# A graph layer with halving weights on one Trainium2 core: one-tile units at both ends, marks chosen per unit, counts alternating with products, and bases by VectorE scans

## The reference

```python
def reference(x, adj, L0_gnn_weight, L0_gnn_bias):      # x (4096, 64), adj (4096, 4096) of 0.0 and 1.0, fp32
    h = jnp.maximum(_layernorm(x, axis=-1), 0.0)
    support = h @ weight                                # (4096, 64)
    mask = (adj != 0).astype(support.dtype)
    rank = jnp.cumsum(mask, axis=1)
    deg = rank[:, -1:]
    k = jnp.minimum(deg, 100.0)
    pos = rank - (deg - k)
    w = mask * jnp.where(pos > 0, 0.5 ** (k - pos), 0.0)
    return x + (w @ support + bias)
```

## Time and profile before

| | before |
|---|---|
| median of 3 runs | 245.06 us (244.77 to 246.62) |
| profiled execution | 244.41 us, its span 242.1 us |
| PE, PEld | 208.9 us (86%), 203.0 us (84%) |
| DVE | 206.9 us (85%) |
| ACT | 170.2 us (70%) |
| POOL | 31.3 us (13%) |
| adjacency loads | 33.56 MB written, 67.1% of the 16 DMA engines' span |
| granted TensorE clock, mean | 0.979 |

### The profile page before, as it was taken

One profiled execution on the slowest core, in us unless ns is written; L12 is line 12 of the kernel. 1 busy time (PEld: TensorE's weight loads), 2 busy tenths in 40 slices (PEclk: granted clock), 3 DMA queues, 4 the chain that ended last, 5 costly groups with the idle time before them and its releaser, 6 DMA issues.

```text
span 242.1 us, 6387 instructions
## 1 busy us (share of the span) xinstructions
PE 208.9 (86%) x2816; PEld 203.0 (84%) x2816; DVE 206.9 (85%) x285; ACT 170.2 (70%) x302; POOL 31.3 (13%) x53
## 2 busy tenths in 40 slices
PE   0530766886999999999999999999999999999993
PEld 0530654776998999999999999999999999999982
DVE  0999979999999999999998999998999995526424
ACT  2411636856687888787888887888887888888640
POOL 8500000004001040104040104030000000000000
PEclk9995699999999999999999999999999999999999
DMA  7999999999999999999999999994000000000000
GB/s 204 191 217 217 195 214 215 215 217 215 217 217 215 218 215 216 218 213 220 214 218 214 218 215 212 214 204 106 0 14 3 11 3 14 0 14 7 6 14 22
DMA packets 7386, 36.11 MB, mean 149 GB/s; under 512 B 1088, under 2 KB 3136, under 8 KB 3136
## 3 DMA queue, kind: packets, MB, share of 16 engines
q0 software_dynamic: 4608, 33.56, 67.1%
q1 hardware_dynamic: 2448, 2.10, 3.1%
q10 hardware_dynamic: 304, 0.07, 0.1%
HBM read 68.22 MB, written 1.05 MB: 286 GB/s over the span
## 4 chain that ended last, share of the span: by engine, by line
PE 68%; DVE 21%; DMA 5%; issue 2%; ACT 1%; POOL 1%; POOLq 0%
PE acc L529 30%; PE chain L511 22%; PE chain L509 10%; DVE masks L292 8%; DMA adj_b<-in_adj 5%; DVE powers L322 3%; PE tot L475 2%; DVE powers L318 2%; DVE part L300 2%; PE chain L490 1%; PE chain L496 1%; DVE sums L310 1%; DVE support L385 1%; ACT powers L257 1%; DVE powers L380 1%
## 5 line engine op out<-in xcount | busy, mean ns | idle before, releaser
L257 ACT ACTIVATE powers<-chain 128x512 int16<-128x512 f32 (+1 forms) x272 | 156.8, 585 | 45.5 <-PE chain L511 27.6
L529 PE MATMUL acc<-support,powers 128*128 128x192 bf16 x1024 | 123.5, 246 | 4.1 <-DVE powers L322 4.0
L509 PE MATMUL chain<-diag_past,masks 128*128 128x128 bf16 x480 | 84.3, 225 | 5.8 <-ACT powers L257 5.7
L511 PE MATMUL chain<-diag_own,masks 128*128 128x128 bf16 x512 | 89.3, 227 | 0.0
L529 PEld LDWEIGHTS acc<-support,powers 128*128 128x128 bf16 x1024 | 82.8, 99 | 5.3 <-DVE powers L322 5.1
L509 PEld LDWEIGHTS chain<-diag_past,masks 128*128 128x128 fp8e3 x480 | 69.0, 148 | 8.7 <-ACT powers L257 8.2
L511 PE MATMUL chain<-diag_step,masks 128*128 128x128 bf16 x512 | 73.7, 226 | 0.0
L292 DVE TENSOR_SCALAR masks<-adj_b 128x4096 uint8<-128x4096 bf16 x32 | 72.6, 2286 | 0.3 <-DMA adj_b<-in_adj 0.2
L511 PEld LDWEIGHTS chain<-diag_own,masks 128*128 128x128 fp8e3 x512 | 68.7, 147 | 0.0
L511 PEld LDWEIGHTS chain<-diag_step,masks 128*128 128x128 fp8e3 x512 | 54.0, 148 | 0.0
L318 DVE TENSOR_SCALAR powers<-powers 128x1024 int16<-128x1024 int16 (+1 forms) x64 | 29.1, 455 | 22.7 <-ACT powers L257 22.7
(11 more groups left out here) (55 smaller groups left out, 88.5 us busy)
## 6 DMA issues: line engine op xcount, KB each, us to landing
adj_b<-in_adj POOLq DMA_DIRECT2D x32, 1024.0 KB, 22.0
x_sb<-in_x SPq DMA_DIRECT2D x1, 1024.0 KB, 5.0
out<-x_sb SPq DMA_DIRECT2D x16, 64.0 KB, 2.9
w<-in_L_gnn_weight ACTq DMA_DIRECT2D x2, 16.0 KB, 4.6
bias_b<-in_L_gnn_bias ACTq DMA_DIRECT2D x1, 32.0 KB, 4.2
```

The source lines that it names most:

```text
L257: nc.scalar.activation(powers[:, c, b, at:].bitcast(i16), chain[c][:, at:], ACT.Relu, bias=(MAX_NEIGH + 1) * STEP).then_inc(powers_ready[c ...
L509: nc.tensor.matmul(chain[c][:, at:at + P], column(u, k, t + 1), diag_past[:, :], start=False, stop=False, skip_group_check=True)
L511: last = nc.tensor.matmul(chain[c][:, at:at + P], column(u, k, t), diag_own[:, :] if marked else diag_step[:, :], start=False, stop=True, ...
L529: last = nc.tensor.matmul(acc[a][:, k * 3 * D:(k + 1) * 3 * D], powers[:, c, s + 1 if marked else s, at:at + P], support[:, t, :, :].rearr ...
```

## The change

It does these things:

- Units differ in size. Units 0, 1, 2 and the last have one tile, the 14 others two. Units 0 and 17 cut their tile in 4 chains of 8 steps. There are 18 units, with tables for the start, the lag of the products (8 to 14 slots) and the number of marked tiles: 20 tiles are marked in all, units 14 and 15 have none, units 0, 1, 2, 3, 5, 8, 11 and 17 have nothing but marked ones. A unit with only marked tiles has no weighing ahead of its first step.
- In a slot PE takes the chain banks in turn: it waits for what the products and the counts need, then issues product, count, product, count. Products lag 11 slots in most units, and differences come in batches of 8 steps, the floor at the beginning of a DVE slot and the subtraction at its end.
- The bases: DVE scans the sums from the end (`scan`, two bytes a result, bf16 out), and one matmul for each chain turns the scanned row into the base. turn_totals, turn_out, the bank `tot` and the constants `ident`, `behind`, `ones`, `unmarked` are gone. POOL clears `sums` and `sums_4`.
- The layer norm: x is loaded in two halves, the rows are normalized ahead of the transposes, and the three parts of support are split without DVE: ACT copies a part out of PSUM, PE subtracts it there with a minus identity (`take_off`), and so on.
- The squares lie in the last of the 7 load buffers, whose load waits for their sum. POOL issues 4 loads ahead of its half of the centring, not 7.

```diff
--- before.py
+++ after.py
-    K = 2
-    H = 2
-    C = K * H
-    STEPS = T // H
-    BEATS = STEPS + 1
-    NU = NT // K
     FLIGHT = 3
-    MARKED = 2
-    BATCH = 4
-    BEHIND = 7
+    BATCH = 8
     LOADS = 7
-    RING = 5
+    RING = 10
...
+    SIZES = [1, 1, 1, 2, 2, 2, 2, 2, 2, 2, 2, 2, 2, 2, 2, 2, 2, 1]
+    CHAINS = [4, 2, 2, 2, 2, 2, 2, 2, 2, 2, 2, 2, 2, 2, 2, 2, 2, 4]
+    STEPS = [T // h for h in CHAINS]
+    MARKS = [1, 1, 1, 2, 1, 2, 1, 1, 2, 1, 1, 2, 1, 1, 0, 0, 1, 1]
+    STARTS = [0, 5, 10, 15, 22, 28, 33, 39, 45, 50, 56, 62, 67, 73, 79, 84, 90, 96]
+    LAGS = [14, 10, 8, 11, 11, 11, 11, 11, 11, 11, 11, 11, 11, 11, 11, 11, 11, 8]
+    NU = len(SIZES)
+    FIRST = [sum(SIZES[:u]) for u in range(NU)]
+    SHIFT = FIRST[SIZES.index(2)] % 2
+    UNIT_OF = [u for u in range(NU) for _ in range(SIZES[u])]
+    TAKEN = [STEPS[u] + (MARKS[u] < SIZES[u]) for u in range(NU)]
...
+        sums = sb("sums", [P, SUMS, 2, 2 * P + 1], u16)
+        sums_4 = sb("sums_4", [P, 1, 4 * P + 1], u16)
+        later = sb("later", [P, SUMS, 2, 2 * P + 1], bf16)
+        later_4 = sb("later_4", [P, 1, 4 * P + 1], bf16)
...
+        sq = adj_b[:, LOADS - 1, :].bitcast(fp32).rearrange("p (t d) -> p t d", d=D)
...
+        turned = (acc[0], acc[1])
+        split = (acc[2], acc[3])
...
+            for f in range(2):
+                sp.dma_start(half_of(x_sb, f), half_of(x.rearrange("(p t) d -> p t d", t=T), f))\
+                  .then_inc(x_loaded[f], 16)
             for u in range(NU):
-                sp.wait_ge(rows_done, u + 1)
-                sp.dma_start(out_p[u], x_sb[:, K * u:K * u + K, :]).then_inc(stored, 16)
+                sp.wait_ge(rows_done[u % ACCS], u // ACCS + 1)
+                rows = slice(FIRST[u], FIRST[u] + SIZES[u])
+                sp.dma_start(out_t[:, rows, :], x_sb[:, rows, :]).then_inc(stored, 16)
...
+                if n == LOADS - 1:
+                    pool.wait_ge(sq_sum_ready, 2)
...
+            for m in (ident_f, minus, diag_own, diag_past, diag_step, diag_base):
...
+            for n in range(4):
                 load(n)
-            pool.wait_ge(mean_ready[1], 1)
-            nc.gpsimd.tensor_tensor(part_of(cen, 1), part_of(x_sb, 1), spread(mean, 1),
+            nc.gpsimd.memset(sums[:, :, :, :], 0.0).then_inc(rests_ready, 1)
+            nc.gpsimd.memset(sums_4[:, :, :], 0.0).then_inc(rests_ready, 1)
+            pool.wait_ge(mean_ready, 2)
...
+            def part(i, s, ready):
+                act.wait_ge(split_ready, 6 * (i // 2) + 2 * s + i % 2 + 1)
+                t = 8 * BLOCKS[i]
+                nc.scalar.activation(support[:, t:t + 8, s, :], split[i % 2][:, :].rearrange("p (t d) -> p t d", d=D),
+                                     ACT.Copy).then_inc(ready, 1)
...
+                if b == 0 and MARKS[u] == SIZES[u]:
+                    return
+                act.wait_ge(chain_ready[c], taken_until(u) + b + 1 - (MARKS[u] == SIZES[u]))
+                cols = slice(0, SIZES[u] * CHAINS[u] * P) if b else plain(u)
...
+                if g == 5:
+                    turn_h(0)
+                    turn_h(1)
+                if g == 6:
+                    part(0, 0, high_ready)
+                    part(1, 0, high_ready)
+                if g == 7:
+                    part(0, 1, middle_ready)
+                    part(1, 1, middle_ready)
                 if g == 8:
-                    high_part(1)
+                    part(0, 2, low_ready)
+                    part(1, 2, low_ready)
...
+                if n >= RING:
+                    u = UNIT_OF[n - RING]
+                    dve.wait_ge(chain_ready[u % FLIGHT], taken_until(u) + TAKEN[u])
...
+            def halve_1(u):
+                n, k = FIRST[u], SIZES[u]
+                at = (n + SHIFT) % RING
+                dve.wait_ge(mask_ready, n + k)
+                halve(u, masks[:, at:at + k, :].rearrange("q k n -> q (k n)").bitcast(u16),
+                      part1[:, 0:k * N // 4].rearrange("q (c t) -> q c t", t=STEPS[u] // 4), STEPS[u] // 4, halved)
+            def halve_2(u):
+                if CHAINS[u] == 4:
+                    return
+                k = SIZES[u]
+                dve.wait_ge(halved, halved_until(u) + 1)
+                halve(u, part1[:, 0:k * N // 4], part2[:, 0:k * N // 8].rearrange("q (c t) -> q c t", t=STEPS[u] // 8),
+                      STEPS[u] // 8, halved)
+            def halve_3(u):
+                k, h = SIZES[u], CHAINS[u]
+                dve.wait_ge(halved, halved_until(u + 1))
+                if u == 0:
+                    dve.wait_ge(rests_ready, 2)
+                if u >= SUMS:
+                    dve.wait_ge(later_ready, FIRST[u - SUMS + 1])
+                at = (part2[:, 0:k * N // 8] if h == 2 else part1[:, 0:k * N // 4])\
+                    .rearrange("q (k c t) -> q k c t", k=k, t=2)
+                nc.vector.tensor_tensor(runs_of(sums, sums_4, u)[:, :, 0:h * P], at[:, :, :, 0], at[:, :, :, 1],
+                                        ALU.add).then_inc(sums_ready, 1)
+            def scan(u, k):
+                dve.wait_ge(sums_ready, u + 1)
+                if k == 0 and u >= SUMS:
+                    dve.wait_ge(chain_ready[(u - SUMS) % FLIGHT], taken_until(u - SUMS) + 1)
+                two = runs_of(sums, sums_4, u)[:, k, :].bitcast(u8).rearrange("q (r e) -> q e r", e=2)
+                nc.vector.tensor_tensor_scan(runs_of(later, later_4, u)[:, k, ::-1], two[:, 0, ::-1], two[:, 1, ::-1],
+                                             (OWN + STEP) / STEP if k < MARKS[u] else 0.0,
+                                             ALU.add, ALU.add).then_inc(later_ready, 1)
...
+            def differ(u, j):
+                c = u % FLIGHT
+                dve.wait_ge(floored[c], batches_until(u) + j + 1)
+                before = powers[:, c, BATCH * j:BATCH * j + BATCH, plain(u)]
+                after = powers[:, c, BATCH * j + 1:BATCH * j + BATCH + 1, plain(u)]
...
+            def normalize(f):
+                dve.wait_ge(ln_step, 6)
+                dve.wait_ge(cen_ready[f], 1)
+                nc.vector.tensor_tensor(half_of(cen, f), half_of(cen, f), spread(rstd, f),
+                                        ALU.mult).then_inc(unit_rows, 1)
...
+            row_sums(0)
+            row_sums(1)
             means(0)
-            dve.wait_ge(mean_ready[0], 1)
-            nc.vector.tensor_tensor(part_of(cen, 0), part_of(x_sb, 0), spread(mean, 0),
-                                    ALU.subtract).then_inc(cen_ready[0], 1)
             means(1)
-            variance(0)
-            prepare(0, 0)
-            deviation(0)
-            scale(0)
-            prepare(0, 1)
-            rest_part(0)
-            prepare(0, 2)
-            low_part(0)
-            prepare(0, 3)
-            prepare(0, 4)
+            center(0)
+            square_sums(0)
+            mask(0)
+            halve_1(0)
+            square_sums(1)
+            halve_2(0)
+            halve_3(0)
+            scan(0, 0)
+            variance()
+            mask(1)
+            halve_1(1)
+            deviation()
+            halve_2(1)
+            halve_3(1)
+            scan(1, 0)
+            normalize(0)
+            mask(2)
+            halve_1(2)
+            normalize(1)
+            halve_2(2)
+            halve_3(2)
+            scan(2, 0)
+            mask(3)
+            add_bias(0)
+            add_bias(1)
+            dve.wait_ge(xb_ready, 2)
             for g in range(SLOTS + 4):
                 for u in range(NU):
-                    if BATCH < g - start(u) <= BEATS and (g - start(u) - 1) % BATCH == 0:
-                        differences(u, (g - start(u) - 1) // BATCH - 1)
-                later_half(g)
+                    if MARKS[u] < SIZES[u] and g - STARTS[u] in range(BATCH + 1, STEPS[u] + 2, BATCH):
+                        floor(u, (g - STARTS[u] - 1) // BATCH - 1)
                 for u in range(NU):
-                    if u and 0 <= g - start(u) + 8 < 5:
-                        prepare(u, g - start(u) + 8)
-                    if 0 <= g - start(u) - STEPS - BEHIND < 3:
-                        combine(u, g - start(u) - STEPS - BEHIND)
+                    to = STARTS[u] - g
+                    if u >= 3 and to == 9 and FIRST[u] > 3:
+                        mask(FIRST[u])
+                    if u >= 3 and to == 7 and SIZES[u] > 1:
+                        mask(FIRST[u] + 1)
+                    if u >= 3 and to == 6:
+                        halve_1(u)
+                    if u >= 3 and to == 5:
+                        halve_2(u)
+                    if u >= 3 and to == 4:
+                        halve_3(u)
+                    if u >= 3 and to == 3:
+                        scan(u, 0)
+                    if u >= 3 and to == 2 and SIZES[u] > 1:
+                        scan(u, 1)
+                    done = STARTS[u] + LAGS[u] + STEPS[u]
+                    if g == done:
+                        add_low(u)
+                    if g == done + 1:
```

(45 more changed lines are left out.)

497 lines of the change are left out of this document (203 added, 294 removed).

## The result

| | before | after |
|---|---|---|
| median of 4 runs beside each other | 244.92 us (244.33 to 246.62) | 232.46 us (231.93 to 233.18) |
| profiled execution, its span | 244.41, 242.1 us | 232.5, 230.1 us |

The ratio is 0.9482 [0.9429, 0.9536]: 12.5 us less. The forecast was 230.5 in a range of 225 to 238. All times are medians that leave out two slow executions, one of 304.31 us at a granted clock of 0.663 (the kernel with unread matmuls) and one of 427.8 us (the kernel before).

What follows compares the result with a forecast made beforehand. Bound before: DVE busy 74.95 of the first 84 us, then PE busy throughout to 228. Start 45.0 + PE work 176.0 + stalls 3.5 + end 3.05 = 227.6 us span; plus 2.95 gives 230.5, range 225 to 238.

Steps and rivals of the forecast that it cites:

- (a): PE: totals leave, 16.0 us in all; the new base is one matmul for each chain, 68 in all, 3.8 us.
- (b): PE: 20 tiles instead of 16 carry marks, so counts go from 1504 to 1620, +7.3 us.
- within one slot of PE: Slots 31 to 93: DVE's 121 us against PE's 122 keep it this close, except where units 14 and 15 lack marks.
- (c): PE: about 850 counts stand behind a product and cost 0.055 us, not 0.063: -4.7 us.
- Rivals 1 and 3: On alternation: 1, hides nothing, +4.7 us, 235 (0.17 with longer start); 3, exposes weight loads, 285 us (0.05 with others).
- rival 4: PE: two counts behind a product go at 0.055 and units 14 and 15's stalls fit: 226 us; 0.10 with shorter start.
- Rival 2: DVE becomes the bound: at 1.2 us net a scan, 22 scans add 13 us to DVE, 240.5 us; chance 0.06.
- Stalls of units 14 and 15: Without marks, slots 88 and 93 need 4.1 and 4.7 us of DVE against PE's 3.3: 3 us of stalls.
- The 0.5 in the last products: At the end, the second batch of unit 16's last products misses by about 0.5 us.
- putting the wait ahead of the products costs nothing: PE blocks: the two other blocks, 1.35 us, cover a chain's 0.92 us round trip through ACT.
- Loads don't bind: Masks need tile n at slot times later than 11.9 + 4.95 n us, so loads set no limit.
- The start: Up to slot 15: normalized rows at 24.4 us, support's two rounds to 41.6, slot 15 at 45.0.

Runs made afterwards that it cites:

- the one with both edits: Units 14 and 15 at lag 12 and products issued first in slots 15 to 27, against the kernel after: 230.94 us, 1.5 us less.

## Why the prediction was right, and where it wasn't

**The balance.** The forecast for the span was 227.6 us and the profiled one 230.1, 2.5 more. By the trace of the kernel after it divides so: slot 15 came 2.0 sooner; PE has gaps of 1.7 us before 112 us, where none were expected (1.2 of them in slots 15 to 28, the rest at 71.9, 94.0 and 110.4); gaps from 176 us on are 3.3 us (2.9 up to 203, 0.4 in the last products) against 3.5; the end behind PE is 0.3 longer; and what is left, 183.7 (43.02 to 226.76) less 5.0 of gaps, is 178.7 us of work against 176.0, 2.7 more. -2.0 + 1.7 - 0.2 + 0.3 + 2.7 = 2.5. The median lies 2.4 above that span, where 2.95 were added, and so 2.0 above the forecast. The closeness is in part luck: the start that came 2.0 us sooner hides as much of the work that was priced too low, and in two other executions, where the clock rose earlier, slot 15 came another 0.6 sooner. Of the signs that the prediction named, 17 slots took 35.1 us (84.74 to 119.84) and not 34.6, and a step with one marked tile about 0.685 and not 0.675.

**(a) Totals and bases.** -16 + 3.8 was right in kind. Eleven matmuls put back in 14 units cost 7.0 of their 8.6 us. From slot 15 on there are 60 base matmuls, not the 64 of the sum, 0.2 us less.

**(b) Marks, +7.3 on PE.** The count of matmuls stands in the trace (596 past counts on L561). What the step lacked is what the marks bring on DVE: it took the differences of four tiles off DVE's work, but the sum has them as a cost of PE alone, with DVE "within one slot of PE". With uniform marks the kernel is 13.6 us slower although PE has fewer matmuls. The statement held for the given table only, and with little to spare.

**(c) Alternation, -4.7.** Mis-sized: 3.3 us. The number of counts behind a product was right (843 from slot 15 on, about 850 predicted), their price wasn't: a pair of counts behind a product takes 0.122 and not 0.118, since the second of it takes 0.066 and not 0.063, and a single one 0.056. All counts from slot 15 on take 91.1 us in the trace and not 88.2 (by the prediction's own prices and 850 such counts the sum is 88.5). With the 0.2 of the bases that is the 2.7 us of work above the sum. The prediction's row has one count behind a product in a step and no pair. The prediction cited the Trainium skill (page "TensorE: Matmul & The Clock Gate", section "The mechanism"), by which weight loads of the same row groups overlap nothing and alternation gives 0. The runs don't agree with that: the loads of the products lie hidden in both orders (0.083 each at 192 columns), and alternation gives 3.3 us. Rivals 1 and 3 are refuted, and rival 4 too: a second count doesn't go at 0.055.

**The scan and DVE.** 0.687 us measured, 0.68 taken. The Trainium skill (page "DVE: opcode table, instruction layouts, handler registers and perf-mode slots", section "Datapath and trigger behaviour") has the scan at half throughput, which the trace bears out: (1.222 - 0.687) / 256 us, 2.09 ns for each further element, from the rows of 513 and 257 elements. That leaves 0.15 us fixed; with the same fixed part the row sums of 1024 elements in 1.22 us run at an estimated 1.04 ns for each, half of that. Of "DVE stays within one slot" the middle part is wrong: at 181 us unit 12's differences, of an ordinary unit, are 1.06 us late. Rival 2's condition (1.2 us net for a scan) didn't hold, but it named the right engine and the right reaction: it had 22 scans of 0.6 us more cost 10 us, and 30 of 0.6 measured 12.6, or 11.7 at the full clock.

**Stalls of units 14 and 15.** 3.0 predicted; the two cost about 1.6 (0.56 and 1.05 by the gaps), and a slot more for them gives 1.1. The sum came out by luck, because the wait of unit 12, 1.2 by its gap, stands beside them. The 0.5 in the last products was 0.4.

**ACT: "putting the wait ahead of the products costs nothing".** This failed in slots 16 to 21. The two other blocks were taken as those of two-tile units, 1.35 us; here they are of one-tile units, and the round trip takes longer than they do. The rule that the prediction gave itself ("with less than 0.92 there it would") was right, and wasn't applied to the slots where the units are small.

**"Loads don't bind".** The pace was right: masks 8 and 10 began at 52.93 and 62.78, 4.93 a tile against 4.95. But the line lies 1.4 us later than 11.9 + 4.95 n, the masks waited for it, and from there it holds unit 6's base with 0.7 us to spare. It doesn't bind this kernel; it took back the gain of the kernel with the products first, and not that of the one with both edits, whose tile 10 landed 0.4 us sooner.

**The start.** The first scan ended at about 17.9 (17.7 predicted), and the centred rows were ready at 24.6 (24.4). The last part of support was there at 40.2, not 41.6, and slots 12 to 14 with their small chains took 2.8 us, not 3.4: a chain of one tile repeats each 0.94 (40.55 to 41.49), not each 1.15. The first products of w took 2.81 us (2.8 taken), their transposes 1.97 (1.7 taken).

**Where the 12.5 us come from.** Undone one at a time, the parts cost: marks 13.6 (a part of it clock), one-tile ends 8.9, the dropped totals 7.0 of 8.6, alternation 3.3. Together that is 32.8, far above 12.5. One reason is that the change has a cost which none of these takes away, the scans: 30 more of them cost 12.6, so those that are there cost an estimated 12 us or so. The rest fits parts that aren't additive: with two engines at 0.98 and 0.96 up to 198 us, whichever of them gets work back becomes late for the other. No run undoes two of the parts together, so this isn't shown.

## What to carry to other kernels

When a second engine is near the bound, price each edit on both engines and unit by unit: the table of marks puts 60 more matmuls on PE than uniform marks do, and is over 10 us quicker because of what it takes off DVE, and when. A round trip that is covered between large blocks must be worked out again wherever the blocks are small. A transfer that seems hidden has a margin (here 0.7 us in one execution), and a quicker start can use it up.

## What the runs showed of the hardware

- A wait of PE of 2.45 us was followed by 3.4 us at a granted clock of 0.51, while others of 1.98 us weren't: the wait's price was 1.6 us above its length.
- Eight of the kernels give PE the same work up to slot 15. The granted clock rose at 27.2 us in two of their executions and at 28.6 to 30.2 in the others; slot 15 began at 42.35 and 42.41 us in the two, and at 42.85 to 44.00 in the others.
- In the kernel after, 128-column matmuls follow one another each 0.107 us at 26.5 to 27.2 us, the lower level, while the windows' granted clock reads 1.00 there. So the spacing of equal matmuls is the surer reading of the clock in this trace.
- The second half of x landed between 6.4 and 8.2 us in eleven executions profiled with this start. Where it came at 8.0 us or later (three of them), the first base stood at 18.98 to 19.12 us, in the others at 17.97 to 18.55.
- Behind a 192-column product a 128-column count takes 0.056 us, and a second count behind it 0.066; counts among themselves take 0.063.
